# Perceiver layer on one core: the gating bias carried by the last channel, the feed-forward residual on TensorE, block maxima by tile

## The reference

```python
def nvfp4_linear(x, w, s_in):
    s_w = fp4_global_scale(w)
    xq = fake_quant_nvfp4(x, s_in)
    wq = fake_quant_nvfp4(w, s_w)
    return jnp.einsum('bsh,oh->bso', xq, wq)
```

## Time and profile before

| | |
|---|---|
| Median of 3 runs | 490.59 us (490.52 to 491.70) |
| Profiled execution, its own time | 490.7 us |
| Its span from first to last instruction | 488.9 us |
| Mean granted TensorE clock | 0.936 |
| Busy: TensorE, VectorE, ScalarE, GpSimd | 388.1, 448.5, 356.0, 15.3 us |
| Moved by DMA | 27.65 MB |

### The profile page before, as it was taken

The page is one execution under the profiler, slowest core; times in us unless marked ns, Lnnn a source line. Parts: engine busy times, 40 slices in busy tenths (PEclk is TensorE's granted clock), DMA queues, the critical chain, the costliest instruction groups (busy, mean ns, idle before and its releaser), DMA issues.

```text
span 488.9 us, 5944 instructions
## 1 busy us (share of the span) xinstructions
PE 388.1 (79%) x1877; PEld 300.9 (62%) x1880; DVE 448.5 (92%) x684; ACT 356.0 (73%) x937; POOL 15.3 (3%) x32
## 2 busy tenths in 40 slices
PE   1997749998988988988988898955999799554563
PEld 1876537777877877877777777855875345112232
DVE  4798999999999999999999999999988687989994
ACT  2569986897897887897887897855459466656643
POOL 4001420000000000000000000000000000000000
PEclk9998879999999999999999999985999999669976
DMA  7952000220220220220220220230200000000001
GB/s 235 359 181 86 0 1 1 87 86 2 86 86 2 86 87 1 87 86 1 87 86 1 86 86 1 62 112 0 87 0 0 1 1 1 0 0 0 23 21 43
DMA packets 27102, 27.65 MB, mean 57 GB/s; under 512 B 1216, under 2 KB 26816, under 8 KB 27072
## 3 DMA queue, kind: packets, MB, share of 16 engines
q1 hardware_dynamic: 26704, 27.27, 17.4%
q0 software_dynamic: 224, 0.01, 0.0%
q10 hardware_dynamic: 144, 0.00, 0.0%
HBM read 26.22 MB, written 1.05 MB: 56 GB/s over the span
## 4 chain that ended last, share of the span: by engine, by line
DVE 68%; PE 16%; issue 9%; ACT 4%; DMA 1%; SPq 0%; ACTq 0%
DVE focus_words L1219 8%; DVE focus_words L1203 8%; PE bank L944 5%; DVE sorted L1242 4%; DVE level L1228 4%; DVE level L1229 4%; DVE merge L1255 4%; DVE sorted L1243 4%; PE bank L772 3%; DVE sorted L1147 3%; DVE amax L1116 2%; DVE sorted L1248 2%; DVE sorted L1247 2%; DVE keymax L1245 2%; DVE merge L1253 2%
## 5 line engine op out<-in xcount | busy, mean ns | idle before, releaser
L772 PE MATMUL bank<-WkT,rows_T 128*128 128x256 f32 x512 | 127.0, 395 | 33.1 <-ACT rows_T L422 33.1
L772 PEld LDWEIGHTS bank<-WkT,rows_T 128*128 128x128 f32 x512 | 96.7, 197 | 50.6 <-ACT rows_T L422 38.8
L866 PE MATMUL bank<-ctx_words,focus_words 128*128 128x257 f32 x512 | 115.7, 384 | 4.9 <-ACT focus_words L513 4.9
L866 PEld LDWEIGHTS bank<-ctx_words,focus_words 128*128 128x128 f32 x512 | 99.8, 198 | 18.3 <-ACT focus_words L513 7.7
L501 ACT ACTIVATE focus_words<-focus_words,shift,ff 128x256 f32<-128x256 f32 x136 | 79.9, 591 | 0.6
L467 ACT ACTIVATE focus_words<-bank 128x256 f32<-128x256 f32 x136 | 50.0, 378 | 26.7 <-PE bank L772 26.7
L513 ACT ACTIVATE focus_words<-focus_words,row_scale 128x256 f32<-128x256 f32 x136 | 56.2, 508 | 11.6 <-DVE row_scale L1221 11.6
L422 ACT ACTIVATE rows_T<-bank 128x512 f32<-128x512 f32 x78 | 44.4, 595 | 23.5 <-PE bank L745 23.5
L1203 DVE SCALAR_TENSOR_TENSOR focus_words<-focus_words,key_and,key_xor 128x2048 int32<-128x2048 int32 x17 | 39.9, 2345 | 1.9 <-ACT focus_words L467 1.9
L745 PE MATMUL bank<-ident,ctx_words 128*128 128x128 f32 x256 | 38.4, 279 | 3.5 <-DMA ctx_words<-in_ctx_dram 2.9
L1286 DVE TENSOR_TENSOR mask<-focus_words,fifth 128x2048 bf16<-128x2048 f32 x17 | 39.0, 2292 | 0.5
(11 more groups left out here) (187 smaller groups left out, 581.5 us busy)
## 6 DMA issues: line engine op xcount, KB each, us to landing
ctx_words<-in_ctx_dram SPq DMA_DIRECT2D x32, 512.0 KB, 3.9
ctx_words<-in_L_ffn_gate_w_dram SPq DMA_DIRECT2D x2, 1024.0 KB, 8.3
ctx_words<-in_L_ffn_up_w_dram SPq DMA_DIRECT2D x2, 1024.0 KB, 8.7
xs<-in_x_dram SPq DMA_DIRECT2D x4, 256.0 KB, 5.0
ctx_words<-in_L_ffn_down_w_dram SPq DMA_DIRECT2D x2, 512.0 KB, 9.5
ctx_words<-in_L_ffn_down_w_dram SPq DMA_DIRECT2D x1, 1024.0 KB, 4.8
out_dram<-xs SPq DMA_DIRECT2D x4, 256.0 KB, 2.1
focus_words<-in_L_attn_W_qkv_dram SPq DMA_DIRECT2D x1, 768.0 KB, 8.3
```

The lines of the kernel that those rows point to most:

```text
L772: ins = pe.matmul(proj_bank[m][:, t * D:(t + 1) * D], rows_T[:, m % 2, 2 * t + k, :], WT[:, k, :], start=(k == 0), stop=(k == KT - 1))
L866: ins = pe.matmul(sum_bank[k][:, 0:GW], heads_half(expo[slot][:, t, :], k), ctx_ring[:, s, t, :], start=(s == 0 and t == 0), stop=(s == PE ...
```

## The change

**Bias.** A normalised row sums to zero over its 256 channels, so its last channel equals minus the sum of the others. `x_hat2` therefore gets only 255 normalised channels and a one in the last (set once by GpSimd), every weight column has its last entry taken off, and the bias row takes the last row of `WattT`. ScalarE subtracts in place on the loaded rows (`take_last_off`, with the sign reversed, in the pairs a = 3 and a = 5), and the sign is put back when the quads are copied (pairs a = 5 and a = 7). The rows of W_qkv and W_gate are no longer loaded and transposed in the front; they are loaded later into the space of `gateT` and `upT`, and their four quads stand in the two pairs named by `ATT_BEHIND`. The 16 bias matmuls, the three bf16 parts and GpSimd's steps for them go. GpSimd loads the bias as one row of 1024 (still two transfers ahead of its memsets) and moves it into `WattT` after group 10's quads.

**Residual.** `weight_scales` also makes `ident_out`, the identity divided by `out_scale`. `down(t)` begins with an f32 matmul of it with x into the same PSUM tile. What finishes the rows is then a scaled copy on ScalarE instead of VectorE's operation: two tiles at once in chunks 0 to 2, single tiles in the last (`finish_tile`). Tile 7 gets another bank than tile 6. The last store is split in two.

**Maxima by tile.** `tile_max(c, u)` takes the block maxima of one tile. The first one of the next chunk stands ahead of hidden(4c+6), the second one at the end; the first `times_fp8` comes ahead of hidden(4c+7). In the last chunk tile 0 is cut, clipped and multiplied before tile 1 begins.

```diff
-QK_QUADS, W_QUADS = 2, 8
+QK_QUADS, ATT_QUADS, W_QUADS = 2, 4, 8
+ATT_BEHIND = (8, 10)
 FFN_OCTS = 6
...
-        w_rows = focus_words[:, T * D:3 * T * D].rearrange("p (r c) -> p r c", r=16)
+        w_rows = focus_words[:, T * D:2 * T * D].rearrange("p (r c) -> p r c", r=8)
+        att_rows = [wT[:, :, :].rearrange("p k c -> p (k c)").bitcast(F32).rearrange("p (r c) -> p r c", c=D)
+                    for wT in (gateT, upT)]
+        bias_row = key_sums[0:1, BATCH - 1:BATCH + 1, :, :].rearrange("p b k c -> p (b k c)")[:, 0:4 * D]
         x_hat = expo[1]
...
-            return (QK_QUADS if n < 2 else W_QUADS) + PAIRS * n + m
+            att = sum(2 for g in ATT_BEHIND if n > g)
+            return (QK_QUADS if n < 2 else ATT_QUADS) + att + PAIRS * n + m
...
+        def att_quad(q):
+            return group_quad(ATT_BEHIND[(q - ATT_QUADS) // 2] + 1, 0) - 2 + q % 2
         def tail_quad(name):
...
             at = 0
-            for w in (Wq, Wk, Wv, Wp, W_qkv, W_gate):
+            for w in (Wq, Wk, Wv, Wp):
                 n = w.shape[0] // P
...
                 context_half(s, s, BACK, back_loaded)
+            att_v = [W_qkv[0:4 * P, :], W_qkv[4 * P:6 * P, :], W_gate]
+            for w, dst in zip(att_v, (att_rows[0], att_rows[1][:, 0:2, :], att_rows[1][:, 2:4, :])):
+                sp.dma_start(dst, w.rearrange("(r p) c -> p r c", p=P)).then_inc(att_rows_loaded, 16)
             for i in range(BATCH - 1):
...
                              w.rearrange("(r p) c -> p r c", p=P)).then_inc(ffn_loaded, 16)
-            for i in range(BATCH):
+            for i in range(CHUNKS - 1):
                 sp.wait_ge(rows_out_ready, i + 1)
                 sp.dma_start(out_v[i], xs[:, 2 * i:2 * i + 2, :]).then_inc(stored, 16)
-            sp.wait_ge(stored, 16 * BATCH)
+            for t in (T - 2, T - 1):
+                sp.wait_ge(rows_out_ready, CHUNKS + t - (T - 2))
+                sp.dma_start(last_v[t], xs[:, t, :]).then_inc(stored, 16)
+            sp.wait_ge(stored, 16 * (CHUNKS + 1))
...
             for b in (b_qkv, b_gate):
-                n = b.shape[0] // (4 * D // P)
-                pool.dma_start(bias_col[at:at + n, :], b.rearrange("(p c) -> p c", p=n)).then_inc(small_loaded, 16)
+                n = b.shape[0]
+                pool.dma_start(bias_row[:, at:at + n], b.rearrange("(a c) -> a c", a=1)).then_inc(small_loaded, 16)
                 at += n
...
             pool.wait_ge(small_loaded, 64)
-            def bias_step(ins):
-                ins.then_inc(bias_steps, 1)
-                bias_done[0] += 1
-                pool.wait_ge(bias_steps, bias_done[0])
-            bias_done = [0]
-            rest = bias_col[:, :]
-            for part in range(3):
-                bias_step(pool.tensor_copy(bias_split[:, part, :], rest))
-                if part < 2:
-                    bias_step(pool.tensor_tensor(bias_left[:, part, :], rest, bias_split[:, part, :], ALU.subtract))
-                    rest = bias_left[:, part, :]
-            for part in range(3):
-                pool.dma_start(bias_parts[part:part + 1, :].rearrange("a (p c) -> a p c", p=P),
-                               bias_split[:, part, :]).then_inc(bias_parts_ready, 16)
+            pool.wait_ge(quad_in_sbuf, group_quad(ATT_BEHIND[1] + 1, 0))
+            pool.dma_start(WattT[P - 1:P, KT - 1, :], bias_row).then_inc(bias_row_ready, 16)
+            pool.wait_ge(expo_ready, CGROUPS + 1)
+            pool.memset(x_hat2[:, :, D - 1:D], 1.0).then_inc(ones_in_last, 1)
-            def evacuate_quad(q, dst_src, free=None):
+            def evacuate_quad(q, dst_src, free=None, scale=1.0):
                 for dst, src in dst_src:
-                    ins = act.activation(dst, src, ACT.Copy)
+                    ins = act.activation(dst, src, ACT.Copy, scale=scale)
                 ins.then_inc(quad_in_sbuf, 1)
-                at = q if q < QK_QUADS else q + 2 * PAIRS
+                at = q if q < QK_QUADS else q + 2 * PAIRS if q < ATT_QUADS else att_quad(q)
                 src = quad_bank[at % 2][:, :].rearrange("p (r k c) -> p r k c", r=2, k=KT)
...
                     pairs = [(dst[:, :, r * P:(r + 1) * P], src[:, r]) for r in range(2)]
-                evacuate_quad(at, pairs)
+                evacuate_quad(at, pairs, scale=-1.0 if q >= ATT_QUADS else 1.0)
+            def take_last_off(part):
+                act.wait_ge(att_rows_loaded, 48)
+                for r in range(PAIRS):
+                    w = att_rows[part][:, r, :]
+                    act.activation(w[:, 0:D - 1], w[:, 0:D - 1], ACT.Identity, scale=-1.0, bias=w[:, D - 1:D])\
+                        .then_inc(last_taken_off, 1)
...
-            def normalise(k, dst):
+            def normalise(k, dst, cols=D):
                 for t in range(T)[NORM_TILES[k]]:
-                    act.activation(dst[:, t, :], xs[:, t, :], ACT.Identity, scale=rstd[:, t:t + 1],
+                    act.activation(dst[:, t, 0:cols], xs[:, t, 0:cols], ACT.Identity, scale=rstd[:, t:t + 1],
                                    bias=shift_ln[:, t:t + 1]).then_inc(x_hat_ready, 1)
...
                 logarithms(a, at(a))
+                if d + 2 in ATT_BEHIND:
+                    take_last_off(ATT_BEHIND.index(d + 2))
                 if last:
...
                     scale_rows(a, at(a))
+                    if d in ATT_BEHIND:
+                        q = ATT_QUADS + 2 * ATT_BEHIND.index(d)
+                        weight_quad(q)
+                        weight_quad(q + 1)
                     lift(d, 2, at(d))
...
             logarithms(0, -1)
-            for q in range(QK_QUADS, W_QUADS):
+            for q in range(QK_QUADS, ATT_QUADS):
                 weight_quad(q)
...
+            def finish_rows(c):
+                act.wait_ge(down_in_psum, 2 * c + 2)
+                act.activation(xs[:, 2 * c:2 * c + 2, :], bank[4 + c % 2][:, :].rearrange("p (t c) -> p t c", t=2), ACT.Copy,
+                               scale=out_scale[:, 2:3]).then_inc(rows_out_ready, 1)
+            def finish_tile(t):
+                act.wait_ge(down_in_psum, t + 1)
+                act.activation(xs[:, t, :], bank[4 + (t + 1) % 2][:, (t % 2) * D:(t % 2 + 1) * D], ACT.Copy,
+                               scale=out_scale[:, 2:3]).then_inc(rows_out_ready, 1)
             def rows_oct(o):
...
                     half_step(5 + 2 * c + u, slice(u * HIDDEN, (u + 1) * HIDDEN))
+                if c:
+                    finish_rows(c - 1)
                 if more:
...
                 hidden_oct(2 * c + 1)
+            finish_tile(T - 2)
+            finish_tile(T - 1)
         def _(pe):
-            pe.wait_ge(consts_ready, 10)
+            pe.wait_ge(consts_ready, 9)
             pe.wait_ge(w_loaded, 32)
...
             project_context(1)
-            pe.wait_ge(w_rest_loaded, 64)
-            for q in range(QK_QUADS, W_QUADS):
+            pe.wait_ge(w_rest_loaded, 32)
+            for q in range(QK_QUADS, ATT_QUADS):
                 transpose_quad(q + 2 * PAIRS, two_tiles(w_rows, q))
...
                     project(d, 3, WkT)
+                    if d in ATT_BEHIND:
+                        part = ATT_BEHIND.index(d)
+                        pe.wait_ge(last_taken_off, PAIRS * part + PAIRS)
+                        for r in range(2):
+                            transpose_quad(att_quad(ATT_QUADS + 2 * part + r), two_tiles(att_rows[part], r))
                 if last:
...
                 pe.wait_ge(x_hat_ready, T + 2 * m + 2)
+                if m == 0:
+                    pe.wait_ge(ones_in_last, 1)
                 transpose_quad(tail_quad(f"xhat{m}"), two_tiles(x_hat2, m))
...
                 for k in range(KT):
-                    pe.matmul(dst, TAIL_ROWS[f"xhat{t // 2}"][:, 2 * (t % 2) + k, :],
-                              WattT[:, k, half * 512:(half + 1) * 512], start=(k == 0), stop=False)
-                ins = pe.matmul(dst, ones_b[:, :], bias_parts[:, half * 512:(half + 1) * 512], start=False, stop=True)
+                    ins = pe.matmul(dst, TAIL_ROWS[f"xhat{t // 2}"][:, 2 * (t % 2) + k, :],
+                                    WattT[:, k, half * 512:(half + 1) * 512], start=(k == 0), stop=(k == KT - 1))
                 if half == 1:
...
                 c = t // 2
+                dst = (bank[4] if t == T - 1 else bank[4 + c % 2])[:, (t % 2) * D:(t % 2 + 1) * D]
                 if c >= 2:
-                    pe.wait_ge(rows_out_ready, c - 1)
+                    pe.wait_ge(rows_out_ready, c - (t < T - 1))
+                pe.matmul(dst, ident_out[:, :], xs[:, t, :], start=True, stop=False)
                 pe.wait_ge(oct_in_sbuf, FFN_OCTS + 2 + t + 1)
                 for k in range(HIDDEN // P):
-                    ins = pe.matmul(bank[4 + c % 2][:, (t % 2) * D:(t % 2 + 1) * D], hid_fp4T[:, t % 2, k, :], downT[:, k, :],
-                                    start=(k == 0), stop=(k == HIDDEN // P - 1))
```

(45 more changed lines are left out.)

27 lines of the change are left out of this document (15 added, 12 removed).

## The result

The change made the kernel 0.8% faster: 487.52 us against 491.67 us for the kernel before on the same chip, ratio 0.9918 with a 95% interval of 0.9903 to 0.9934, about 4 us. The forecast was 481.5, with a range of 479.3 to 484.8. One further run took 987 us, for a reason not known, and does not enter the ratio. The profiled execution took 487.39 us (span 485.6, mean granted clock 0.944).

A forecast was written before the change was run, and what follows sets the result against it. VectorE bounds the main-loop pairs, TensorE the gating stage, mostly VectorE the chunks. Terms -1.86 + 0.45 - 3.68 - 3.46 - 0.6 = -9.15 took the profiled 490.7 to 481.55, forecast 481.5 us, range 479.3 to 484.8.

The forecast's parts named there:

- Another wait takes the start-up gap: Rival, start-up: the load of group 2's rows or ScalarE waiting on TensorE fills the gap; 483.4 us, chance 0.10.
- Start-up, -1.86: Before the main loop: four weight-transpose quads leave the front, so VectorE's whole gap before the first reciprocal goes, -1.86 us.
- Main loop, 0: Pairs of context groups: ScalarE's added subtractions and evacuations fit its waits, and GpSimd's changed work delays nobody; 0 us.
- The cover: Main loop: ScalarE's wait of 1.98 us absorbs its added work; rival that this fails costs 3 to 6 us, chance 0.05.
- Scales, +0.45: In weight_scales: an added reciprocal and 128x128 multiply stand ahead of mix(2), all on the path, +0.45 us.
- Gating stage, -3.68: Gating stage: sixteen bias matmuls go, saving 0.80 us up to the last TensorE run and 2.88 in it, -3.68 us.
- clock rival: Gating stage: TensorE's clock halves for some 4 us (483.5 us, chance 0.10) or throughout (504 us, chance 0.03).
- Chunks, -3.46: Feed-forward chunks: finish_rows leaves VectorE and half the block maximum fills silu waits; -1.37, -1.09 and -1.0, sum -3.46 us.
- ScalarE's copies did not come late: Rival, chunks: copies delay silu and hidden(4c+6), so only finish_rows' own time is won; 483.0 us, chance 0.10.
- the -2.0 that the forecast gave to `finish_rows` alone: Chunks: the smaller bound, with only the time of finish_rows won, -2.0 us.
- End, -0.6: After the last chunk: tile-by-tile cutting, a shorter ScalarE copy and a halved store, -0.6 us; +0.9 at half clock throughout.

The follow-up runs named there:

- e1: The kernel after, with one small GpSimd multiply of 128x8 on a scratch tile added behind the all-reduce: 481.81 us, ratio 0.9796 to the kernel before.
- e2: The kernel before, with GpSimd's bias steps and their three transfers moved ahead of the all-reduce: 498.82 us, ratio 1.0148.
- g1: The kernel after plus the small GpSimd multiply behind the all-reduce, with the identity's reciprocal and multiply moved ahead of gating tile 2: 481.07 us, ratio 0.9792.
- f3: The kernel before with only the residual part changed, block maxima over a whole chunk and the last chunk's cut as before: 492.5 us, ratio 1.001.
- f1: The kernel before with only the bias part of the change, plus the small GpSimd operation behind the all-reduce: 485.58 us, ratio 0.9879.
- g4: The kernel after, with the small GpSimd operation as GpSimd's very last one, behind the memset of ones: 481.58 us.

## Why the prediction missed

The step that failed is this sentence of the main loop's part: "On GpSimd five small operations and three transfers go, for which nobody waited, and one transfer and a memset of 128x8 come, each long before its reader: 0." It counted the instructions and their readers. What it did not ask was what the removed operations left behind. The subtractions were the only operations of their kind behind the all-reduce. Without them the idle time that stood in front of the first one (6.64 us, nobody waiting) moved into the next execution, in front of the first `affine_select`, where TensorE, ScalarE and VectorE all wait for the constants. There it was 9.11 us long, and the load of Wk covered part of it. The measured price is 5.7 us against e1 (first reciprocal 48.15 against 42.45, of which 5.39 stand at the first transposes and 0.30 are the first projection's; medians 487.52 and 481.81), and 5.69 against the kernel before at the first transposes. (`make_keys` of group 0 is 6.64 later than before. That this equals the idle time behind the all-reduce is chance: 0.95 of it is not GpSimd's.) With this one term the forecast would have been 481.5 + 5.7 = 487.2. The hole in the trace of before could be read: 6.64 us that end with "issue" on an engine that nobody waits for. I passed over it since it cost nothing. That it would reach into the next execution no row of before says; that took e1 and e2.

None of the rivals named this either. "Another wait takes the start-up gap" was priced at the 1.86 itself, as if that were the most that the front could lose.

The steps one by one, forecast and measured:

- **Start-up, -1.86**: the gap went in every kernel without the early quads. First reciprocal 41.47, 41.68, 42.04, 42.23, 42.31, 42.45 in those six without the hole (mean 42.03), and 43.45, 43.68, 44.26, 44.52 in the four with them (mean 43.98): -1.95. What is left of the spread inside each group follows the first projection (below). The mechanism held and was buried under the later constants.
- **Main loop, 0**: 298.76 against 298.79, and no wait of VectorE in it. The cover held: ScalarE's wait before `rows_T` shrank from 1.98 to 1.08.
- **Scales, +0.45**: +0.40 (and g1 takes it back).
- **Gating stage, -3.68**: tile 0's wait from 1.52 to 0.62, -0.91 where -0.80 was forecast; tile 7 another -3.05 where -2.88 was. With the 0.40 the stretch is 3.57 shorter. The granted clock stayed at 1.00 (the third number from the end in the window of the kernel after), and neither clock rival came.

```profile
391.50:418.50 27.00, 25.81 (x124) 14.28 (x123) 22.00 (x57) 19.39 (x29) 0.00 (x0) 1.00 0.01 2
```

- **Chunks, -3.46**: -3.96. Successive scalings are 12.84, 12.55 and 12.55 apart, where 14.22, 13.90 and 13.78 were. Chunk 0 came as forecast (-1.38); in chunks 1 and 2 (-1.35, -1.23) no wait was left where I had kept 0.25. ScalarE's copies did not come late. In f3, without the maxima by tile, the residual gave nothing in the chunks, so the -2.0 that the forecast gave to `finish_rows` alone was nothing by itself.
- **End, -0.6**: -0.37. The chain after shows why not more: TensorE at half its clock until 482, as was feared for part of the stretch.

```profile
478.66 0.86 PE bank L1043 x2
479.52 1.71 PE bank L1046 x8
481.23 0.85 PE bank L1043 x2
482.08 0.94 PE bank L1046 x8
```

The identity took 0.86 and the eight of tile 6 1.71 for the 1.3 assumed, the second identity 0.85 for 0.43; the copy and the half store gave more than the 0.3 taken: from the last operation's start to the end 2.56, before 3.29 (485.61 to 488.9). A half store landed in 1.7 against 2.1. That 0.4 is near the 0.3 which followed as an estimate from the Trainium skill (DMA: Bandwidth & Descriptors, "Anatomy of one DMA"), though that section fits transfers issued by GpSimd, and this store is SP's. Its sum is too high here: with its fixed 2.0 the estimate for the two stores is 2.3 and 2.6, and 1.7 is less than the fixed part alone.

Without the failed term the sum was near: -9.15 forecast, span -8.8 in e1 and -10.1 in g1.

**The first projection.** Its eight matmuls of 128x256 took between 1.99 and 2.93 us in these kernels (before 1.99, e1 2.63, after 2.93), which moves the first reciprocal by up to 1 us:

```profile
13.63 1.99 PE L772 MATMUL bank<-WqT,rows_T 128*128 128x256 f32 x8
```

```profile
19.33 2.93 PE L808 MATMUL bank<-WqT,rows_T 128*128 128x256 f32 x8
```

It is TensorE's clock, as I had put it in what I expected of f1. The windows print 1.00 for the front only because the trace has no record of the clock there. The first record, of 1.00, begins at 13.46 in the kernel before, at 15.25 in e1 and at 21.26 in the kernel after, in the last two amid these eight. Up to it single matmuls start 0.43 apart, behind it 0.22, half and full speed. All fourteen profiles agree: the later the record begins after the projection's start, the longer the eight take. TensorE was idle up to its first transposes (9.54 before, 15.23 after). So this 1 us belongs neither to the change nor to GpSimd's hole.

**Open.** What GpSimd lacks behind an all-reduce, and why the hole is 6.6 us long in one place and 11.2 in another, was not shown.

## What to carry to other kernels

Before removing the last operations of an engine, read every idle time of that engine that ends with "issue", also where nobody waits for it, and ask what the removed work had been paying for; the next execution starts in the state that this one leaves. Here one multiply of 128x8 behind the all-reduce is worth 5.7 us. A wait of the other engines in front, here for the load of Wk, hides part of such a loss. And an operation taken off the bounding engine just ahead of a wait is worth nothing until something else fills the wait: move work into it first, then count the gain.

## What the hardware showed unexpectedly

GpSimd stood still for 6.6 to 7.6 us behind an all-reduce before its next `tensor_tensor` (6.64, 6.89, 6.94, 7.10, 7.29, 7.30, 7.35, 7.54, 7.55), and for 9.1 to 11.2 us before the first `affine_select` where in the previous execution neither of the two kinds ran behind the all-reduce (9.11, 10.21, 10.66, 11.19). A cast of 128x8 right behind the all-reduce started at once in the kernel before (48.74) but took 1.17, where the same cast ahead of the all-reduce took 0.18 in e2. The Trainium skill (GPSIMD Engine Reference, "Instruction dispatch") says that the first call to a freshly loaded GpSimd kernel pays about 6 us for its code, which no profiled instruction shows. The runs here agree in kind and show more, 6.6 to 11.2. The page doesn't say that the loss carries over into the next execution; the runs of e1, e2 and g4 show it. The long ones fall into a front where the DMA is busy, windows of the kernel after and of e1:

```profile
5.00:13.00 8.00, 0.00 (x0) 0.00 (x0) 6.53 (x27) 0.42 (x2) 0.00 (x0) 1.00 0.97 328
```

```profile
48.00:55.00 7.00, 3.53 (x24) 2.95 (x24) 6.97 (x10) 6.53 (x19) 0.00 (x0) 1.00 0.37 124
```

Share 0.97 and 328 GB/s in front, 0.37 and 124 behind the all-reduce. In g4 the hole stands where nothing is moved, and it is 7.29 long all the same:

```profile
337.00:344.00 7.00, 7.00 (x30) 6.21 (x30) 6.86 (x15) 0.35 (x1) 0.01 (x1) 0.84 0.00 0
```

So traffic doesn't make the hole. That it lengthens it in front is a guess; no run separated traffic from place.
